# Four feed-forward mixtures of a cross-attention stack: routing, look-ahead and weight spreading rewritten

## The chip, the cores and the metric

The kernel runs on one core of one Trainium2 chip. The metric is device time in microseconds of one execution, the median of several runs. A profiled execution of the same program gives the trace; its own time is named beside it, since every duration below is read from that one execution. Six parts of the core are named: TensorE (PE in the rows, with PEld for its weight loads), VectorE (DVE), ScalarE (ACT), GpSimd (POOL), SyncE (SP), and the DMA queues.

## What is computed

The reference sends 2048 tokens of 128 numbers (x, 8 sequences of 256, float32) through four layers. Each layer is a cross-attention to a context of 8 x 1601 rows, then a feed-forward part; the fourth also has a self-attention in its feed-forward part. The change touches only the four feed-forward mixtures. Three of them are alike:

```python
scores = sigmoid(y @ router_w.T)          # y: the layer norm of x, 16 experts
s = scores + bias                         # 4 groups of 4 experts
# keep the two groups whose two best experts sum highest, then the four best experts in them
w = scores[chosen] / (sum(scores[chosen]) + 1e-20) * SCALE
out = sum over chosen e of  w[e] * (act(y @ gate[e]) * (y @ up[e])) @ down[e]  +  shared part
```

Layer 0 has hidden width 128 per expert and a shared part of 256, layer 1 has 32 and 256, layer 2 has 64 and 128; layers 0 and 1 use silu(gate) * up, layer 2 the square of relu without an up matrix. The fourth takes the one best of 8 experts:

```python
one_hot = one_hot(argmax(y @ gate_w + gate_b))
h = gelu(einsum('td,edh->teh', y, w1))    # hidden 512 per expert
out = einsum('te,ted->td', one_hot, einsum('teh,ehd->ted', h, w2))
```

## The kernel before

The program is nine phases, one behind the other, and each ends before the next begins: L0a, L0f, L1a, L1f, L2a, L2f, L3a, L3s, L3f. The names ending in f are the mixtures. A phase is one block with an instruction list of its own for each engine and its own semaphores, which are cleared behind it (L60). Nothing outside the four mixtures is touched.

A mixture is described by an `Experts` object (L2448) and emitted by `build_experts` (L2494). The tokens are four chunks of 512, each of four token tiles of 128. All weights stay in SBUF, transposed so that an expert's hidden units lie on the 128 partitions. A chunk is worked hidden tile by hidden tile: 18 hidden tiles in L0f (16 routed, 2 shared), 6 in L1f (4 and 2), 9 in L2f (8 and 1), 32 in L3f (4 for each of 8 experts). From here on "tile" is such a hidden tile of 128 units by 512 tokens, one PSUM bank.

For each tile PE makes the first-layer product into `hp` (and the up product into `up`) as three fp32r products, high x high, low x high and high x low (`three`, L2624 to L2626), ACT applies silu, relu or gelu (`hidden`, L2759), DVE multiplies by up (L2969) and by the expert's weight (L2974; L2981 and L2983 in L2f), and PE adds the second-layer product into `yp` as one plain fp32 product (`down`, L2674), which the trace counts as two instructions. PE runs one tile ahead: products(q+1), weigh(q+1), down(q). When a chunk is finished, ACT copies `yp` to `ft` (L2765), PE turns it back (L2620), DVE adds x (L3000) and SP stores it.

The expert's weight is a number per token and has to stand in all 128 partitions. It is cut into three bf16 parts (`cparts`, L2941 to L2946), turned by PE (L2613), copied to `ct` (48 rows: 3 parts of 16 experts, L2951) and spread by a product of `sel` with `ct`, a contraction over 48 rows (`weigh`, L2657; in L3f over 8 rows, `mask`, L2665, applied to the tokens ahead of the first layer by `only`, L2958 and L2959).

Routing of a chunk: DVE takes statistics (L2797 and L2800), an inverse root by shifts and Newton steps of small DVE instructions (L70 to L82, L2808), ACT norms (L2722), PE turns (L2599), ACT copies twice, plain and rounded (L2732, L2733), DVE makes the low part (L2814), PE makes the logits (L2606), ACT the sigmoid (L2741), and DVE picks groups and experts in some 40 small instructions (L2849 to L2946). L1f and L2f route all four chunks first. L0f and L3f route chunk 0 first and the other three beside the tiles of chunk 0, step by step in the order of the table `beside`. The weights are split into high (ACT, L2747 and L2749) and low parts (DVE, L2819 and L2822) before their first use. The order on each engine is the order in which the code is written.

## Time and profile before

| what | us |
|---|---|
| median of three runs (4938.65 to 4943.12) | 4939.88 |
| the profiled execution | 4936.75 |
| its span | 4935.0 |
| TensorE busy in the span | 4338.2 (88%) |
| VectorE, ScalarE, GpSimd busy | 2831.2, 2570.1, 32.7 |
| mean granted TensorE clock, share of full | 0.935 |
| L0f, L1f, L2f, L3f (first transfer to the copy of the last chunk) | 264.9, 126.7, 143.3, 262.0 |

The mixtures begin at 260.9, 1288.0, 3084.1 and 4665.7. Together they are 797 of 4935 us; the attention phases hold the rest. Within a mixture the engines hand tiles to one another, so what sets its length is read from the order of starts on PE, not from the busy shares. In the rows, `128x512 f32` behind a name is the shape of the output, `<-` reads "made from" (or, in brackets, "waited for"), and `x4` counts instructions.

### The profile page before, as it was taken

What the parts mean: (1) busy time and instruction counts of PE and PEld (TensorE: products, weight loads), DVE (VectorE), ACT (ScalarE), POOL (GpSimd) and SP (SyncE); (2) the same over time, 40 slices, a digit from 0 to 9 for tenths busy, and PEclk for the clock granted to TensorE, in tenths of its full rate; (3) what the DMA queues carried; (4) which work ended last, traced back from release to release, by engine and by line L of the source; (5) the groups of instructions that cost most, each with busy time, mean ns of one, the idle gap of its engine ahead of it and who ended that gap; (6) DMA issues with size and microseconds to landing.
All of it is one profiled execution on the core that took longest, in us unless ns stands there. A gap on an engine that the chain in (4) does not pass through costs nothing. (4 is left out here: it accounts for less than half of the span.)

```text
span 4935.0 us, 76710 instructions
## 1 busy us (share of the span) xinstructions
PE 4338.2 (88%) x27172; PEld 2929.8 (59%) x27172; DVE 2831.2 (57%) x7008; ACT 2570.1 (52%) x4392; POOL 32.7 (1%) x23
## 2 busy tenths in 40 slices
PE   3869799999579999999899998669999999967699
PEld 3635444545357777777677776346666666644455
DVE  6654688888355666556565564555555555447531
ACT  4532377767327666666666665234444444336433
POOL 0000000000000000000000000000000000000000
PEclk8879799999689999999999999789999999988899
DMA  1110143331010000000000000010000000000100
GB/s 46 27 44 7 60 61 45 53 48 28 23 50 2 13 11 6 12 5 13 13 4 11 3 3 2 25 52 9 7 9 8 8 2 2 2 18 4 59 3 7
DMA packets 115142, 99.36 MB, mean 20 GB/s; under 512 B 11480, under 2 KB 106872, under 8 KB 113648
## 3 DMA queue, kind: packets, MB, share of 16 engines
q1 hardware_dynamic: 108992, 87.35, 8.1%
q10 hardware_dynamic: 5760, 6.92, 0.4%
q8 instruction: 232, 3.80, 0.3%
q14 instruction: 158, 1.29, 0.1%
HBM read 62.91 MB, written 12.58 MB: 15 GB/s over the span
## 5 line engine op out<-in xcount | busy, mean ns | idle before, releaser
L1240 DVE CUSTOM_DVE_ANT_0 L2a_sc<-L2a_score,L2a_mask_n 128x804 f32<-128x804 f32 x512 | 499.0, 991 | 105.5 <-issue 82.0
L1157 ACT ACTIVATE L2a_pt<-L2a_ring 128x512 f32<-128x512 f32 x768 | 430.6, 598 | 215.6 <-PE L2a_ring L1054 213.6
L621 ACT ACTIVATE L1a_work<-L1a_ring 128x1024 f32<-128x1024 f32 x416 | 413.3, 1026 | 167.4 <-PE L1a_ring L439 166.9
L741 DVE TENSOR_REDUCE L1a_mx<-L1a_ring 128x2 f32<-128x1024 f32 x384 | 456.6, 1222 | 59.8 <-PE L1a_ring L458 56.0
L2178 PE MATMUL L3a_res<-L3a_probs,L3a_n 128*128 128x512 f32 (+1 forms) x960 | 489.6, 592 | 0.0
L2286 ACT ACTIVATE L3a_probs<-L3a_ring 128x512 f32<-128x512 f32 (+1 forms) x480 | 280.1, 590 | 380.5 <-PE L3a_ring L2069 375.9
L1054 PE MATMUL L2a_ring<-L2a_ident,L2a_sc 128*128 128x128 f32 x3072 | 440.8, 282 | 5.5 <-ACT L2a_sc L1144 1.9
L1144 ACT ACTIVATE L2a_sc<-L2a_sc,L2a_nb 128x1608 f32<-128x1608 f32 x256 | 417.2, 1632 | 0.7 <-DVE L2a_nb L1245 0.7
L2392 DVE TENSOR_REDUCE L3a_mx<-L3a_ring 128x1 f32<-128x402 f32 (+2 forms) x640 | 315.6, 538 | 142.9 <-PE L3a_ring L2147 135.2
L1054 PEld LDWEIGHTS L2a_ring<-L2a_ident,L2a_sc 128*128 128x128 f32 x3072 | 347.2, 143 | 81.0 <-issue 44.4
L1069 PE MATMUL L2a_res<-L2a_pt,L2a_v 128*64 128x256 f32 (+1 forms) x3328 | 373.4, 381 | 1.6 <-ACT L2a_pt L1157 1.6
L1265 DVE SCALAR_TENSOR_TENSOR L2a_k_lo<-L2a_ring,L2a_bk,L2a_k_hi 128x402 fp32r<-128x402 f32 x256 | 161.2, 635 | 328.0 <-ACT L2a_k_hi L1176 326.9
L2067 PE MATMUL L3a_ring<-L3a_q_hi,L3a_kt_hi 128*128 128x512 f32 (+1 forms) x480 | 317.4, 661 | 16.6 <-DVE L3a_q_lo L2405 16.6
L1069 PEld LDWEIGHTS L2a_res<-L2a_pt,L2a_v 128*64 128x64 f32 (+1 forms) x3328 | 233.8, 137 | 133.3 <-issue 20.3
L1037 PE MATMUL L2a_score<-L2a_k_hi,L2a_q_hi 64*128 64x402 f32 x1024 | 211.0, 403 | 51.0 <-DVE L2a_mx L1240 36.6
L479 PE MATMUL L1a_res<-L1a_work,L1a_v 128*32 128x256 f32 (+1 forms) x3328 | 229.0, 390 | 3.2 <-ACT L1a_oraw L625 1.7
L1176 ACT ACTIVATE L2a_k_hi<-L2a_ring,L2a_bk 128x402 fp32r<-128x402 f32 x256 | 152.3, 598 | 130.7 <-PE L2a_ring L1018 128.0
L458 PE MATMUL L1a_ring<-L1a_keys,L1a_queries 64*128 64x512 f32 (+1 forms) x1024 | 199.9, 418 | 13.3 <-DVE L1a_mx L741 11.7
L439 PE MATMUL L1a_ring<-L1a_shifted,L1a_keys 64*128 64x512 f32 x832 | 189.3, 462 | 11.4 <-issue 5.8
L2068 PE MATMUL L3a_ring<-L3a_q_lo,L3a_kt_hi 128*128 128x512 f32 (+1 forms) x480 | 189.3, 394 | 0.0
L2069 PE MATMUL L3a_ring<-L3a_q_hi,L3a_kt_lo 128*128 128x512 f32 (+1 forms) x480 | 189.3, 394 | 0.0
L1037 PE MATMUL L2a_score<-L2a_k_hi,L2a_q_lo 64*128 64x402 f32 x1024 | 186.1, 352 | 0.0
(726 smaller groups left out, 8170.7 us busy)
## 6 DMA issues: line engine op xcount, KB each, us to landing
L1a_keys<-L1a_k_hi SPq DMA_DIRECT2D x224, 52.0 KB
...
```

Of the source, the lines that this page charges most:

```text
L621: act.activation(probs[:, (par * NU + u) % c.PS, :, :], ring[tile][:, :, :], ACT.Exp).then_inc(tile_free[tile], 1)
L741: dve.tensor_reduce(mx[:, g % 2, hf, one, :, ch], ring[tile][:, :, :], AX, ALU.max).then_inc(tile_free[tile], 1)
L1037: mm = pe.matmul(score[e][:, k, 0:CH], mine[rows, p % 2, q], theirs[rows, p % 2, w], start=(i == 0), stop=(i == 2))
L1054: mm = pe.transpose(bank[:, t * P:(t + 1) * P], sc[:, r % 2, g // 3, at:at + P], ident[:, :])
L1069: mm = pe.matmul(res[e * DH:(e + 1) * DH, 0:S], v[0:rows, t, h * DH:(h + 1) * DH], pt[0:rows, t, e, :], start=(t == 0), stop=(t == CT - 1))
L1144: act.activation(sc[:, r % 2, e, :], sc[:, r % 2, e, :], ACT.Exp, bias=nb[:, r % 2, e:e + 1], scale=1.0, accum_out=sums[:, r // 2 % 2, r % ...
L1157: ins = act.activation(pt[:, t:t + 4, g // 3, q], bank[:, :].rearrange("p (t q) -> p t q", t=4), ACT.Copy)
L1240: dve.tensor_tensor_reduce(sc[:, two, e, w].rearrange("p (k j) -> p k j", k=2), score[e][:, :, 0:CH], mask_n[:, r % 2, w].rearrange("p (k ...
L2067: pe.matmul(out, hi, m_hi, start=True, stop=False)
L2178: pe.matmul(res[s][:, 0:W], n[0:r, b % c.n_bufs, t, :], probs[0:r, (u * T + i) % c.PS, 0:W], start=first, stop=last).then_inc(pv_ok, 1)
L2286: free(act.activation(probs[0:r, at % c.PS, 0:W], bank[0:r, 0:W], ACT.Exp), "scores", k)
L2392: free(dve.tensor_reduce(mx[:, u % 2, part, to:to + 1], bank[:, 0:valid(s, ch)], AX, ALU.max), "tops", k)
```

## The change

- All 16 token tiles are routed at once before the first weight is spread, in L0f too. Statistics, norm and turns run chunk behind chunk; the turns go to four different PSUM banks, and the 16 logits products follow together.
- The layer norm's inverse root goes from DVE to GpSimd: an add and a power of -0.5 for each chunk (`rsqrt_chunk`). The norm goes from ACT to DVE as a subtract and multiply.
- PE makes the first-layer products of nine tiles (A = 9) before the first spread. DVE's gating multiplies for these nine stand between the routing steps and write into a ring `hid` of 11 tiles; the multiply by the weight follows in place later. L2f has four `hp` banks.
- The first 18 tiles of L0f and 12 of L1f and L2f use plain fp32 products (`w1`, `wu`, `yt`), the others the three fp32r ones, so the splitting comes later.
- `cparts`, `ct` and `sel` have 128 rows, zeroed by GpSimd, so a spread contracts over 128 rows.
- In the weights' scale two DVE instructions become one. The table of the activation function is loaded by a one-column activation ahead.
- L3f has a class and a function of their own (`Single`, `build_single`): three tiles ahead, four `hp` banks, small transfers ahead of `w1`, each chunk's norm and turn beside chunk 0, and from chunk 1 on the second layer as three fp32r products, for which ACT applies gelu twice (rounded to `hid_hi` and plain) and DVE makes `hid_lo`.

```diff
+def rsqrt_chunk(pool, st, half, span):
+    pool.tensor_scalar(st["var"][:, span], st["mv"][:, span, 1], EPS, None, ALU.add)
+    pool.drain()
+    return pool.tensor_tensor(st["rs"][:, span], st["var"][:, span], half[:, span], ALU.pow)
+def norm_chunk(dve, y, x, st, tiles):
+    for t in tiles:
+        ins = dve.tensor_scalar(y[:, t, :], x[:, t, :], st["mv"][:, t, 0:1], st["rs"][:, t:t + 1], ALU.subtract, ALU.mult)
...
-        sel_f, sel = sb("sel_f", [3 * E, c.SEL, P]), sb("sel", [3 * E, c.SEL, P], BF16)
+        sel_f, sel = sb("sel_f", [W, c.SEL, P]), sb("sel", [P, c.SEL, P], BF16)
-        g1, hid = sb("g1", [P, 2, CHUNK]), sb("hid", [P, 2, CHUNK])
+        g1, hid = sb("g1", [P, 2, CHUNK]), sb("hid", [P, R, CHUNK])
...
+            pe.wait_ge(c_in, 16 * 3)
+            for n in range(CN):
+                turn(n)
+            logits()
+            for q in range(A):
+                products(q)
+            parts(0)
+            parts(1)
+            weigh(0)
             for q in range(Q):
-                if q + 1 < Q:
-                    products(q + 1)
-                    weigh(q + 1)
+                if q + A < Q:
+                    products(q + A)
+                if q + 1 < Q:
+                    weigh(q + 1)
                 down(q)
...
+                if plain:
+                    pe.matmul(hp[q % NB][:, :], w1[:, k, :], yt[:, n, :], start=True, stop=True).then_inc(hp_ok, 1)
-                pe.matmul(wp[q % 2][:, :], sel[0:W, k // c.share, :], ct[:, n, :], start=True, stop=True).then_inc(wp_ok, 1)
+                pe.matmul(wp[(r - 1) % 2][:, :], sel[:, k // c.share, :], ct[:, n, :], start=True, stop=True).then_inc(wp_ok, 1)
...
+            groups()
+            gate(0)
+            second()
+            gate(1)
+            keep()
+            gate(2)
...
+            cast()
+            for q in range(7, A):
+                gate(q)
+            parts(0)
+            parts(1)
+            hidden(0)
+            for q in range(Q):
+                if q + A < Q:
+                    gate(q + A)
+                if q + 1 < Q:
+                    hidden(q + 1)
...
+                if n == 0:
+                    pe.wait_ge(hid_ok, q + 1)
+                    pe.matmul(yp[:, :], w2[:, k, :], hid[:, q % 2, :], start=first, stop=last).then_inc(dn_ok, 1)
+                    return
+                pe.wait_ge(lo_ok, q - KC + 1)
+                pe.matmul(yp[:, :], w2_hi[:, k, :], hid_hi[:, q % R, :], start=first, stop=False)
+                pe.matmul(yp[:, :], w2_lo[:, k, :], hid_hi[:, q % R, :], start=False, stop=False)
+                pe.matmul(yp[:, :], w2_hi[:, k, :], hid_lo[:, q % R, :], start=False, stop=last).then_inc(dn_ok, 1)
```

On PE, from the logits of L0f's first chunk to its first down product (`misc` is a PSUM bank for turns and logits, `w` the gate and down weights), the order before was:

```order
L2606 MATMUL L0f_misc<-L0f_wr,L0f_yt 128x16 x4
L2624 MATMUL L0f_hp<-L0f_yt_hi,L0f_w_hi 128x512
L2625 MATMUL L0f_hp<-L0f_yt_hi,L0f_w_lo 128x512
L2626 MATMUL L0f_hp<-L0f_yt_lo,L0f_w_hi 128x512
L2624 MATMUL L0f_up<-L0f_yt_hi,L0f_wu_hi 128x512
...
L2613 MATMUL L0f_misc<-L0f_ident_b,L0f_cparts 48x128 x4
L2657 MATMUL L0f_wp<-L0f_ct,L0f_sel 128x512
...
L2657 MATMUL L0f_wp<-L0f_ct,L0f_sel 128x512
L2674 MATMUL L0f_yp<-L0f_hid,L0f_w 128x512
```

and in the changed kernel:

```order
L2588 MATMUL L0f_misc<-L0f_wr,L0f_yt 128x16 x16
L2623 MATMUL L0f_hp<-L0f_yt,L0f_w 128x512
L2629 MATMUL L0f_up<-L0f_yt,L0f_wu 128x512
...
L2594 MATMUL L0f_misc<-L0f_ident_b,L0f_cparts 128x128 x8
L2594 MATMUL L0f_yp<-L0f_ident_b,L0f_cparts 128x128 x8
L2642 MATMUL L0f_wp<-L0f_ct,L0f_sel 128x512
L2623 MATMUL L0f_hp<-L0f_yt,L0f_w 128x512
L2629 MATMUL L0f_up<-L0f_yt,L0f_wu 128x512
L2642 MATMUL L0f_wp<-L0f_ct,L0f_sel 128x512
L2655 MATMUL L0f_yp<-L0f_hid,L0f_w 128x512
```

The logits of all four chunks, nine tiles' products (the dots stand for eight further pairs) and all 16 turns of the parts now stand ahead of the first spread, and each first-layer product is one instruction in place of three; nine tiles lie between a tile's products and its down product.

On DVE, in L0f's routing (`choice` to `gsum` are the group sums, `g` is ACT's output), the order before was:

```order
L2849 TENSOR_TENSOR L0f_choice<-L0f_score,L0f_rb 128x64
...
L2862 TENSOR_TENSOR L0f_gsum<-L0f_first,L0f_two 128x16
L2868 TENSOR_TENSOR L0f_g_large<-L0f_gsum 128x8
...
L2969 TENSOR_TENSOR L0f_hid<-L0f_up,L0f_g 128x512
L2974 TENSOR_TENSOR L0f_hid<-L0f_wp,L0f_hid 128x512
```

and in the changed kernel:

```order
L2789 TENSOR_TENSOR L0f_choice<-L0f_score,L0f_rb 128x256
...
L2801 TENSOR_TENSOR L0f_gsum<-L0f_first,L0f_two 128x64
L2869 TENSOR_TENSOR L0f_hid<-L0f_up,L0f_g 128x512
L2806 TENSOR_TENSOR L0f_g_large<-L0f_gsum 128x32
...
L2812 TENSOR_TENSOR L0f_thr<-L0f_thr,L0f_wsum 128x16
L2869 TENSOR_TENSOR L0f_hid<-L0f_up,L0f_g 128x512
L2774 TENSOR_TENSOR L0f_g_above<-L0f_gsum,L0f_thr 128x64
```

The routing steps now work on all 16 token tiles at once (256 columns for 64), the gating multiply of one tile stands behind each of them, and the multiply by the weight follows elsewhere.

On PE, in L3f's loop (before: chunk 0, the later chunks alike; `ym` the masked tokens), the order before was:

```order
L2665 MATMUL L3f_wp<-L3f_ct,L3f_sel 128x512
L2674 MATMUL L3f_yp<-L3f_hid,L3f_w 128x512
L2624 MATMUL L3f_hp<-L3f_ym_hi,L3f_w_hi 128x512
L2625 MATMUL L3f_hp<-L3f_ym_hi,L3f_w_lo 128x512
L2626 MATMUL L3f_hp<-L3f_ym_lo,L3f_w_hi 128x512
```

and in the changed kernel, in chunk 1:

```order
L3090 MATMUL L3f_hp<-L3f_ym_hi,L3f_w_hi 128x512
L3091 MATMUL L3f_hp<-L3f_ym_hi,L3f_w_lo 128x512
L3092 MATMUL L3f_hp<-L3f_ym_lo,L3f_w_hi 128x512
L3078 MATMUL L3f_wp<-L3f_ct,L3f_sel 128x512
L3108 MATMUL L3f_yp<-L3f_hid_hi,L3f_w_hi 128x512
L3109 MATMUL L3f_yp<-L3f_hid_hi,L3f_w_lo 128x512
L3110 MATMUL L3f_yp<-L3f_hid_lo,L3f_w_hi 128x512
```

The down product is three fp32r products from the rounded and the low part of `hid`.

## Rows read from the trace of the kernel before

**Rows 1.** the four phases by stretch: length, then busy PE, PEld, DVE, ACT, POOL; clock; DMA

```profile
255.00:531.00 276.00, 222.68 (x728) 126.55 (x727) 137.12 (x328) 71.27 (x118) 0.00 (x0) 0.88 0.07 23
1285.00:1420.00 135.00, 82.61 (x288) 51.10 (x288) 58.65 (x172) 32.51 (x64) 0.00 (x0) 0.74 0.09 26
3081.00:3234.00 153.00, 94.48 (x292) 48.62 (x292) 78.01 (x197) 37.81 (x72) 0.00 (x0) 0.76 0.08 24
4663.00:4935.00 272.00, 231.33 (x752) 130.58 (x752) 68.96 (x163) 95.33 (x164) 0.00 (x0) 0.93 0.09 28
```

**Rows 2.** the copy of each finished chunk: ns min/median/max, first to last start

```profile
L2765 ACT ACTIVATE L0f_ft<-L0f_yp x4: 597/598/598, 377.6 to 525.8; 128x512 f32<-128x512 f32 x4
...
L2765 ACT ACTIVATE L1f_ft<-L1f_yp x4: 597/598/598, 1365.8 to 1414.7; 128x512 f32<-128x512 f32 x4
...
L2765 ACT ACTIVATE L2f_ft<-L2f_yp x4: 597/598/600, 3166.5 to 3227.4; 128x512 f32<-128x512 f32 x4
...
L2765 ACT ACTIVATE L3f_ft<-L3f_yp x4: 598/598/599, 4765.5 to 4927.7; 128x512 f32<-128x512 f32 x4
```

**Rows 3.** one tile of L0f on PE, with and without the spread (start, us)

```profile
443.57 0.39 PE L2626 MATMUL L0f_up<-L0f_yt_lo,L0f_wu_hi 128*128 128x512 f32 x1
443.89 0.39 PE L2657 MATMUL L0f_wp<-L0f_ct,L0f_sel 48*128 48x512 bf16 x1
...
445.40 0.40 PE L2625 MATMUL L0f_hp<-L0f_yt_hi,L0f_w_lo 128*128 128x512 f32 x1
...
471.17 0.39 PE L2626 MATMUL L0f_up<-L0f_yt_lo,L0f_wu_hi 128*128 128x512 f32 x1
471.40 1.02 PE L2674 MATMUL L0f_yp<-L0f_hid,L0f_w 128*128 128x512 f32 x2
...
472.49 0.40 PE L2625 MATMUL L0f_hp<-L0f_yt_hi,L0f_w_lo 128*128 128x512 f32 x1
```

**Rows 4.** the token tiles' transfers and statistics in L0f, L1f and L2f

```profile
L2576 SPq DMA_DIRECT2D L0f_x<-x_L0a x3: 428/507/527, 261.9 to 262.9; - x3
...
DMA to landing us min/median/max: 2.9/9.7/11.4
...
L2797 DVE BATCH_NORM_STATS2 L1f_st_six<-L1f_x x16: 274/276/295, 1293.4 to 1298.9; 128x6 f32<-128x128 f32 x16
...
L2797 DVE BATCH_NORM_STATS2 L2f_st_six<-L2f_x x16: 275/278/294, 3090.0 to 3095.5; 128x6 f32<-128x128 f32 x16
```

**Rows 5.** timeline rows of the setup and routing, and L101 by its line

```profile
4675.81 0.23 DVE L3015 CAST L3f_ident_b<-L3f_ident 128x128 bf16<-128x128 f32 x1 [9.67 <-DMA L3f_bx<-in_L3f_bx]
...
4680.54 0.16 DVE L2808 SCALAR_TENSOR_TENSOR L3f_st_off<-L3f_st_mv,L3f_st_rs 128x4 f32<-128x4 f32 x1
...
L101 DVE TENSOR_SCALAR L2a_xn<-L2a_xin,L2a_st_mv,L2a_st_rs x16: 341/342/346, 1441.5 to 2777.6; 128x128 f32<-128x128 f32 x16
...
1311.33 1.86 PE L2606 MATMUL L1f_misc<-L1f_wr,L1f_yt 128*128 128x16 f32 x8 [5.10 <-ACT L1f_yt_hi L2733]
...
1327.34 0.42 DVE L2849 TENSOR_TENSOR L1f_choice<-L1f_score,L1f_rb 128x256 f32<-128x256 f32 x1 [1.57 <-ACT L1f_score L2741]
...
1342.66 0.29 DVE L2946 CAST L1f_cparts<-L1f_comb 128x256 bf16<-128x256 f32 x1
```

**Rows 6.** one turn of the chain in L2f, all engines

```profile
3181.17 0.40 PE L2626 MATMUL L2f_hp<-L2f_yt_lo,L2f_w_hi 128*128 128x512 f32 x1
...
3181.61 0.60 ACT L2759 ACTIVATE L2f_g<-L2f_hp 128x512 f32<-128x512 f32 x1 [1.47 <-PE L2f_hp L2626]
...
3182.24 0.69 DVE L2981 TENSOR_TENSOR L2f_hid<-L2f_wp,L2f_g 128x512 f32<-128x512 f32 x1 [0.60 <-ACT L2f_g L2759]
```

**Rows 7.** L3f, the down product of its second tile on PE

```profile
4701.71 1.02 PE L2674 MATMUL L3f_yp<-L3f_hid,L3f_w 128*128 128x512 f32 x2
```

**Rows 8.** the stretch in which L1f routes, columns as in Rows 1

```profile
1320.00:1345.00 25.00, 8.77 (x34) 6.77 (x34) 15.09 (x62) 5.05 (x11) 0.00 (x0) 0.50 0.00 0
```

**Rows 9.** the costliest GpSimd instruction of the program, by line

```profile
L669 POOL TENSOR_TENSOR L1a_rq_wide<-L1a_rq,L1a_one 128x1024 f32<-128x1024 f32 x8 | 15.2, 1906 | 721.8 <-DVE L1a_rq L768 721.8
```

More of the change, by code:

```diff
@@ L2456, in __init__ @@
         self.share = max(1, routed // E)
-        self.PARTS = 1 if top1 else 3
-        self.batches = [(0, N_CHUNK)] if second is None else [(0, 1), (1, N_CHUNK)]
-        self.pieces = [(0, 2), (2, (2 + tiles) // 2), ((2 + tiles) // 2, tiles)]
-        chunks = range(1, N_CHUNK)
-        steps = [("stats", n) for n in chunks] + [("rsqrt", 1)] + [("norm", n) for n in chunks]
-        for n in chunks:
-            steps += [("turn", n), ("logits", n)]
-        steps += [(s, 1) for s in (("best", "cast") if top1 else ("groups", "second", "keep", "masked", "top", "pick", "weights",
-                                                                 "cast"))]
@@ L2466, in __init__ @@
-        steps += [("parts", n) for n in chunks]
-        self.beside = {q: [] for q in range(tiles)}
-        if second is not None:
-            for i, s in enumerate(steps):
-                self.beside[1 + i * (tiles - 3) // (len(steps) - 1)].append(s)
-        self.misc = []
-        for c0, c1 in self.batches[:1]:
-            for n in range(c0, c1):
-                self.misc += [("turn", n), ("logits", n)]
-            self.misc += [("parts", n) for n in range(c0, c1)]
-        for q in range(N_CHUNK * tiles):
-            n, k = divmod(q, tiles)
-            if k == 1 and n:
-                self.misc.append(("back", n - 1))
-            if n == 0:
-                self.misc += [s for s in self.beside[k] if s[0] in ("turn", "logits", "parts")]
@@ L2482, in __init__ @@
-        self.misc.append(("back", N_CHUNK - 1))
+        self.pieces = [(k, min(k + 6, tiles)) for k in range(0, tiles, 6)]
+        self.NF = plain // tiles
+        self.matrices = 2 if act == "silu" else 1
+        self.lows = [("low", i) for i in range(len(self.pieces))] + [("turn_lo", n) for n in range(self.NF, N_CHUNK)]
 EXPERTS = {
-    "L0f": Experts("L0f", 16, 18, 16, "silu", fill=-1.0, scale=2.5, second=True),
-    "L1f": Experts("L1f", 16, 6, 4, "silu", fill=LOWEST),
-    "L2f": Experts("L2f", 16, 9, 8, "relu2", fill=0.0, scale=2.5),
@@ L2489, with stats_chunk @@
-    "L3f": Experts("L3f", 8, 32, 32, "gelu", top1=True, second=True),
+    "L0f": Experts("L0f", 16, 18, 16, "silu", -1.0, 2.5, 9, 18),
+    "L1f": Experts("L1f", 16, 6, 4, "silu", LOWEST, 1.0, 9, 12),
+    "L2f": Experts("L2f", 16, 9, 8, "relu2", 0.0, 2.5, 9, 12),
 }
 G = 4
-def build_experts(nc, c, io, x_in, x_out, x_more=None):
-    E, KC, KR, CN = c.E, c.KC, c.KR, N_CHUNK
+def stats_chunk(dve, x, st, tiles):
+    for t in tiles:
+        dve.bn_stats(st["six"][:, t, :], x[:, t, :])
+    dve.drain()
+    for t in tiles:
+        ins = dve.bn_aggr(st["mv"][:, t, :], st["six"][:, t, :])
+    return ins
@@ L2558, in build_experts @@
         span_of = lambda n: slice(n * CTILES, (n + 1) * CTILES)
[L2559 to L2568 removed]
+        routed = lambda q: q % KC < KR
+        routed_to = lambda q: sum(1 for r in range(q + 1) if routed(r))
+        piece_of = lambda k: next(i for i, (p0, p1) in enumerate(c.pieces) if p0 <= k < p1)
         block = done.enter_context(nc.Block())
@@ L3003, in finish, with residual @@
                 dve.nop().then_inc(xo_ok, 1)
-            steps = dict(stats=stats, rsqrt=rsqrt, turn=turn, groups=groups, second=second, keep=keep, masked=masked_of, top=top,
-                         pick=pick, weights=weights, best=best, cast=cast, parts=parts)
+            def residual(n):
+                dve.wait_ge(more_in, 16 * CN)
+                dve.tensor_tensor(more[:, span_of(n), :], more[:, span_of(n), :], x[:, span_of(n), :], ALU.add)
+            steps = dict(stats=stats, norm=norm, turn=turn, best=best, parts=parts)
             dve.memset(seg[:, :, :], 1.0)
```

887 lines of the change are left out of this document (548 added, 339 removed).

## The prediction, made before the changed kernel was run

> **What bounds the kernel now.** I read the stretches of the four phases first [rows 1]. They show where PE is short of work: in L0f it is busy 222.7 of 276 us, in L3f 231.3 of 272, but in L1f only 82.6 of 135 and in L2f 94.5 of 153, at granted clocks of 0.74 and 0.76. No other engine comes near its stretch in L1f (DVE 58.7). So there are two kinds of time: a head, in which one engine waits for the next until routing is done, and a body, in which PE (L0f, L3f) or the chain ACT-DVE-PE (L2f) sets the pace. Then the copies that end each chunk [rows 2]: they fix the end of each phase's PE work (525.8, 1414.7, 3227.4, 4927.7) and of L0f's and L3f's first chunk (377.6, 4765.5). I forecast each phase's last down product against these ends; what follows it (copy, turn, add, store) is the same before and after. Last come single tiles on PE [rows 3], the head's rows [rows 4, 5] and the chain [rows 6].
>
> **Prices on PE at full clock** [rows 3]. One fp32r product: 471.17 to 471.40, 0.23; three are 0.69. From the last up product of one tile to the second product of the next takes 472.49 - 471.17 = 1.32 without a spread, which leaves 1.32 - 2 x 0.23 = 0.86 for a plain fp32 product. The same stretch with a spread takes 445.40 - 443.57 = 1.83, so the spread over 48 rows costs 0.51, more than twice an fp32r product of as many columns. A gated routed tile is 1.38 + 0.51 + 0.86 = 2.75 before. Chunks 1 to 3 of L0f come out at 16 x 2.75 + 2 x 2.24 + about 1.5 for turning back = 50.0 each, and the rows give (525.8 - 377.6) / 3 = 49.4 [rows 2], so the prices hold.
>
> **The spread over 128 rows.** No row of before has a bf16 product of 128 rows beside fp32r ones. Nearest from below: 0.23, as any 512-column product. From above: 0.51, unchanged, if the step between number types is what costs it and not the step between row heights. I take 0.23, because the plain down product (also another type) shows no such extra in [rows 3]. The Trainium skill, "TensorEngine Tiling (Array Packing)", section Key Properties, says that a change of tiling mode drains the TensorE; it would explain 0.51 and its removal, and no row of before shows a 48-row product without the change. By that rule the sum is the one below, without it the rival B.
>
> **The head.** The changed DVE list runs four statistics and four norms before the last turn. Statistics: 5.5 us from the first to the last start of four chunks [rows 4], some 1.6 a chunk with the copy and its drain that the change drops, so 1.35. Norm on DVE: 16 instructions of 0.34 on the same shape [rows 5], 1.2 a chunk against some 1.9 on ACT. Inverse root: on DVE it lies between 4675.81 and 4680.54, where twelve small instructions and the statistics take 4.7 [rows 5]; on GpSimd I take under 1 us, hidden for all but the first chunk, with no row of that operation (bounds: 0.3, and the 1.9 of a 1024-column multiply [rows 9]; a price beyond these is rival D). The logits, four times 1.86 at the low clock [rows 5], are 7.4, and turn and copy of the last chunk 1.1. So the logits are done x1 + 1.35 + 4.8 + 2.7 + 0.25 + 1.1 + 7.4 = x1 + 17.6, with x1 the landing of the second chunk's tokens. Choice to last cast for 16 tiles takes 1342.66 + 0.29 - 1327.34 = 15.6 [rows 5]; the change leaves out one of these steps (0.25) and adds seven gating multiplies of about 0.65, and the sigmoid 0.5. I add 1.6 for DVE waiting on cold products: a plain pair at half clock is 2 x 1.72 = 3.4 and a routing step with its gate about 2.9, L1f being granted 0.50 while it routes [rows 8]. Two sets of turned parts and copies take 2.2. PE then runs on end from F = x1 + 41.9. The high and low parts of the weights now lie beside this; DVE and ACT have room, since a tile takes 1.4 and 0.6 of them against PE's 2.5.
>
> **L0f.** x1: issued from 261.9, landing after 9.7 [rows 4], 271.6, so F = 313.5. Left on PE: 9 plain tiles 15.5, 54 tiles at 1.38 = 74.5, 72 down products 61.9, 63 spreads 14.5, three turns back 1.5, and 1.8 of small gaps: 169.7. End 483.2 against 525.6: **-42.4**. Of it 17.6 (63 x 0.28) is from the spreads; the rest is chunk 0, which ended 377.6 - 261.9 = 115.7 after the tokens' issue, where another chunk took 49.4 [rows 2, 4].
>
> **L1f.** Chunk 0's statistics began at 1293.4 [rows 4]; the second chunk is issued a microsecond later, x1 = 1294.4, F = 1336.3. Left: 3 plain tiles 5.2, 12 x 1.38 = 16.6, 24 x 0.86 = 20.6, 15 spreads 3.5, 1.8 for turns and gaps: 47.7. End 1384.0 against 1414.5: **-30.5**.
>
> **L2f.** x1 = 3090.0 - 0.1 by the same reading, F = 3131.8. Here PE has 1.8 a tile, and a chain is longer: from the start of the last product's pass at 3181.17 ACT starts 0.44 later, DVE 0.63 after that [rows 6]; gate and weight multiply are 0.69 each with drains, so 2.4 from the pass's end to the down product, then 0.86 and 0.69 on PE. That round of 3.93 serves two tiles, since two gates are always under way: 1.96 a tile. 27 tiles so make 53.1, the last nine at about 1.1 (0.86 + 0.23) 9.9, turns and a cold start 2.6: 65.6. End 3197.4 against 3227.2: **-29.8**.
>
> **L3f.** Before, the first instruction waits 9.67 for a 512-byte transfer queued behind w1 [rows 5], and the second down product starts at 4701.71 [rows 7]. After, small transfers go first (I take 4 sooner), statistics and root lie ahead of that landing (4.7), the norm is 0.7 shorter, and two conversions leave the path (1.8): 11.2 earlier. Chunk 0 loses about 6 us of stalls with four hp banks and three tiles ahead, so it ends at 4748.3 instead of 4765.4: -17.1. Chunks 1 to 3: 32 x (0.69 + 0.69) + 8 x 0.23 + 0.5 = 46.5 each, less 2.1 at the end where no products are left: 137.4 against 162.2 [rows 2]: -24.8. ACT's two gelus take 1.2 and DVE 1.0 a tile, both under 1.44, so they stay hidden; a tile more than that would show. Together **-41.9**.
>
> **Sum.** 42.4 + 30.5 + 29.8 + 41.9 = 144.6. Five semaphores more in each of three phases to clear cost about 0.7: -143.9. The profiled execution took 4936.75, its span 4935.0, so 4792.8; the median lies 3.1 above that execution: 4796.
>
> **The rivals.** (A) As above, 4796; single prices move it between 4782 and 4812. (B) The 128-row spread keeps its 0.51: 63 x 0.28 in L0f, 15 in L1f, some 3 us in L2f where a chain hides part of it, and 32 in L3f make 34: 4829. For it: bf16 stands beside fp32r in either kernel. Against it: the plain product's own switch is free. (C) PE is granted half its clock through head and early body, since it is idle between the nine products: L1f's 0.50 while routing [rows 8] speaks for it, L0f's 0.88 [rows 1] against it. Plain tiles at 3.4 would make DVE wait 0.5 at each of seven gates and the products after F slow at first; 4 to 5 us in each of four phases: 4812 to 4816. (D) Slower than before: the power on GpSimd. With p us a call, three phases wait about 4p - 5 longer each and L3f p - 1, together 13p - 16. It takes back 144 us from p = 12.3 on, 4940 and more. GpSimd's only shown price is 1.9 for 1024 columns [rows 9], and this has four. The Trainium skill, "GPSIMD Engine Reference", section Instruction dispatch, gives about 6 us once for the first call of a freshly loaded kernel; here that would fall into the wait for x. (E) The head is shorter than my stalls and the body without gaps: 4778. (F) A cover fails and the look-ahead doesn't help (say DVE's ring waits tie it to PE): only the spreads and L3f are gained, about 4885.
>
> **How the numbers follow.** A 0.60, B 0.15, C 0.12, E 0.07, F 0.03, D 0.03. The range 4771 to 4836 takes in A, B, C and E. A measurement of this kernel can tell about 0.2% (10 us) from no change. Faster by more than that are A, B, C, E and F, 0.97; slower is D from 12.3 us a call, of which I leave 0.02; within 0.2% 0.01.
>
> **What would show it.** In the changed trace: L0f's chunks 1 to 3 between copies at about 45 us (16 x 2.47 + 2 x 2.24 + 1.5) where B gives 49.5; from the last up pass to the down product's start over a spread 0.46 where B gives 0.6 to 0.7; the first down product at about 313, 1336 less the earlier phase's gain, and so on; L2f's down products every 1.96 on the mean; L3f's every 1.44, its ACT never waited for. GpSimd's power under 1 us. Wrong would be the forecast above all if the head of L1f and L2f, where I claim half their gain, waits for something that no row here shows: the second batch of turns on `yp` and `wp`, the table loads, or the zeroing of `cparts` by GpSimd.

## The result and the profile after

The changed kernel takes 4788.05 us (median of 4 runs, 4786.25 to 4795.74), the kernel before 4939.37 beside it (4938.65 to 4943.12). The ratio is 0.9695, 95% interval [0.9678, 0.9712]: 151 us or 3.1% faster. Forecast were 4796 and a range of 4771 to 4836. The profiled execution took 4788.48, its span is 4786.7.

The stretches of [rows 1] begin 3 to 6 us before their mixture and end 5 to 7 after its last copy. Cut to the mixtures themselves, from the first transfer to the last copy, they read in the kernel before (length, then busy time of PE, PEld, DVE, ACT and POOL, granted clock, DMA share, GB/s):

```profile
260.90:525.80 264.90, 221.05 (x716) 125.36 (x716) 135.23 (x323) 70.67 (x117) 0.00 (x0) 0.88 0.07 23
1288.00:1414.70 126.70, 81.95 (x284) 50.68 (x284) 57.96 (x171) 31.92 (x63) 0.00 (x0) 0.74 0.08 26
3084.10:3227.40 143.30, 93.82 (x288) 48.20 (x288) 77.32 (x196) 37.25 (x72) 0.00 (x0) 0.76 0.08 24
4665.70:4927.70 262.00, 230.67 (x748) 130.17 (x748) 68.27 (x162) 94.77 (x164) 0.00 (x0) 0.93 0.09 28
```

and in the changed one:

```profile
261.30:480.90 219.60, 199.01 (x669) 116.56 (x680) 127.19 (x261) 56.05 (x92) 9.03 (x12) 0.92 0.09 27
1247.10:1344.80 97.70, 79.58 (x257) 45.12 (x260) 56.20 (x160) 24.12 (x40) 7.72 (x12) 0.84 0.11 33
3001.80:3117.10 115.30, 87.38 (x272) 45.91 (x276) 75.78 (x189) 30.04 (x52) 8.18 (x12) 0.84 0.10 29
4553.40:4779.40 226.00, 205.97 (x829) 150.12 (x844) 134.46 (x246) 139.40 (x250) 7.90 (x12) 0.94 0.10 33
```

PE's busy time in L0f fell from 221.1 to 199.0 us, but the phase fell more, from 264.9 to 219.6: PE now works 91% of it in place of 83%. In L1f it is 81% in place of 65%, in L2f 76% in place of 65%, and the granted clock of the two rose from 0.74 and 0.76 to 0.84. In L3f PE's share rose least, from 88% to 91%.

The changed kernel's issue of the first token transfer of each mixture (ns, then start), and below it the copies of the finished chunks, which answer to [rows 2]:

```profile
L2564 SPq DMA_DIRECT2D L0f_x<-x_L0a x1: 363/363/363, 261.3 to 261.3; - x1
...
L2564 SPq DMA_DIRECT2D L1f_x<-x_L1a x1: 382/382/382, 1247.1 to 1247.1; - x1
...
L2564 SPq DMA_DIRECT2D L2f_x<-x_L2a x1: 378/378/378, 3001.8 to 3001.8; - x1
...
L3024 SPq DMA_DIRECT2D L3f_x<-x_L3s x1: 359/359/359, 4553.4 to 4553.4; - x1
```

The copies, ns min/median/max, then first to last start:

```profile
L2708 ACT ACTIVATE L0f_ft<-L0f_yp x4: 597/599/599, 359.3 to 480.9; 128x512 f32<-128x512 f32 x4
...
L2708 ACT ACTIVATE L1f_ft<-L1f_yp x4: 597/598/604, 1310.7 to 1344.8; 128x512 f32<-128x512 f32 x4
...
L2708 ACT ACTIVATE L2f_ft<-L2f_yp x4: 597/598/599, 3068.6 to 3117.1; 128x512 f32<-128x512 f32 x4
...
L3181 ACT ACTIVATE L3f_ft<-L3f_yp x4: 597/604/617, 4641.8 to 4779.4; 128x512 f32<-128x512 f32 x4
```

From first transfer to the last chunk's copy L0f takes 480.9 - 261.3 = 219.6 us, where it took 525.8 - 260.9 = 264.9; the others follow in the table.

| gain, us | forecast | measured |
|---|---|---|
| L0f: 264.9 to 219.6 | 42.4 | 45.3 |
| L1f: 126.7 to 97.7 | 30.5 | 29.0 |
| L2f: 143.3 to 115.3 | 29.8 | 28.0 |
| L3f: 262.0 to 226.0 | 41.9 | 36.0 |
| the four together | 144.6 | 138.3 |
| all that lies between and around them | -0.7 | 10.0 |
| spans: 4935.0 to 4786.7 | 143.9 | 148.3 |

So the sum came out 4 us short, by two errors that partly cancel: the mixtures gained 6 less than forecast, which is L3f's miss, since the errors of the other three nearly cancel among themselves, and what the change doesn't touch became 10 shorter. The experiments take up both.

### The profile page after: what moved, and what is told of

It reads as the page before. It is cut to its first block and busy times, and to the rows that moved or that the text cites. A ratio compares the mean times of both kernels' runs of the same rounds, so it can differ in the third digit from the quotient of the medians.

```text
span 4786.7 us, 76756 instructions
## 1 busy us (share of the span) xinstructions
PE 4280.6 (89%) x27163; PEld 2929.6 (61%) x27196; DVE 2885.7 (60%) x7012; ACT 2585.6 (54%) x4410; POOL 65.6 (1%) x71
## 5 line engine op out<-in xcount | busy, mean ns | idle before, releaser
L1037 PE MATMUL L2a_score<-L2a_k_hi,L2a_q_hi 64*128 64x402 f32 x1024 | 207.3, 396 | 41.9 <-DVE L2a_mx L1240 35.6
L2178 PEld LDWEIGHTS L3a_res<-L3a_probs,L3a_n 128*128 128x128 f32 (+1 forms) x960 | 175.2, 189 | 18.0 <-issue 1.0
```

Of the source, the lines that this page charges most:

```text
L2178: pe.matmul(res[s][:, 0:W], n[0:r, b % c.n_bufs, t, :], probs[0:r, (u * T + i) % c.PS, 0:W], start=first, stop=last).then_inc(pv_ok, 1)
```

## The spread over 128 rows

One tile of L0f on PE in the changed kernel, with its spread (`wp`), answering to the first three rows of [rows 3]:

```profile
360.27 0.40 PE L2608 MATMUL L0f_up<-L0f_yt_lo,L0f_wu_hi 128*128 128x512 f32 x1
360.51 0.39 PE L2642 MATMUL L0f_wp<-L0f_ct,L0f_sel 128*128 128x512 bf16 x1
360.74 1.02 PE L2655 MATMUL L0f_yp<-L0f_hid,L0f_w 128*128 128x512 f32 x2
...
361.83 0.39 PE L2607 MATMUL L0f_hp<-L0f_yt_hi,L0f_w_lo 128*128 128x512 f32 x1
```

The spread now takes 0.23 (360.51 to 360.74), as the fp32r products of 512 columns beside it do. From the last up product to the second product of the next tile it is 361.83 - 360.27 = 1.56, where it was 1.83 with the same instructions. Two experiments take the change apart. Most experiments had one run; their readings rest on the lengths of the phases in the trace.

**The changed kernel with 48 rows again.**

```diff
-                pe.matmul(wp[(r - 1) % 2][:, :], sel[:, k // c.share, :], ct[:, n, :], start=True, stop=True).then_inc(wp_ok, 1)
+                pe.matmul(wp[(r - 1) % 2][:, :], sel[0:W, k // c.share, :], ct[0:W, n, :], start=True, stop=True).then_inc(wp_ok, 1)
...
-                pe.matmul(wp[u % 2][:, :], sel[:, e, :], ct[:, n, :], start=True, stop=True).then_inc(wp_ok, 1)
+                pe.matmul(wp[u % 2][:, :], sel[0:E, e, :], ct[0:E, n, :], start=True, stop=True).then_inc(wp_ok, 1)
```

> The changed kernel, but each spread contracts over 48 rows again (8 in L3f); everything else stays. Theory: the height of the contraction costs 0.28 us a spread where PE sets the pace, so L0f is longer by 63 x 0.28 = 17.6 us, L1f by 15 x 0.28 = 4.2, L3f by up to 32 x 0.28 = 9 and L2f by 0 to 3, together 31 to 34. Rival: the changed surroundings of the spread (look-ahead) made it short, and the height costs nothing: under 3 us in all.

One tile of L0f on PE in this kernel, start and length in us, with its 48-row spread:

```profile
400.03 0.39 PE L2608 MATMUL L0f_up<-L0f_yt_lo,L0f_wu_hi 128*128 128x512 f32 x1
400.35 0.39 PE L2642 MATMUL L0f_wp<-L0f_ct,L0f_sel 48*128 48x512 bf16 x1
400.67 1.12 PE L2655 MATMUL L0f_yp<-L0f_hid,L0f_w 128*128 128x512 f32 x2
...
401.87 0.40 PE L2607 MATMUL L0f_hp<-L0f_yt_hi,L0f_w_lo 128*128 128x512 f32 x1
```

It took 4824.2 us in one run, 36 more than the changed kernel. By phase: L0f 236.8 (+17.2), L1f 101.6 (+3.9), L2f 118.1 (+2.8), L3f 232.6 (+6.6), together 30.5, just under the 31 expected; the rest is in L1a, of which more below. In the rows of PE the price has three parts: 0.32 ahead of the spread and 0.32 behind it, in place of 0.23 or 0.24 each, and 401.87 - 400.67 = 1.20 in place of 1.09 from the down product on. So PE loses about a tenth of a microsecond at each of the two crossings between heights and another tenth on the product behind the second.

**The kernel before with 128 rows only.**

```diff
-        sel_f, sel = sb("sel_f", [3 * E, c.SEL, P]), sb("sel", [3 * E, c.SEL, P], BF16)
+        sel_f, sel = sb("sel_f", [3 * E, c.SEL, P]), sb("sel", [P, c.SEL, P], BF16)
...
-        ct = sb("ct", [W, CN, CHUNK], BF16)
+        ct = sb("ct", [P, CN, CHUNK], BF16)
...
-                pe.matmul(wp[q % 2][:, :], sel[0:W, k // c.share, :], ct[:, n, :], start=True, stop=True).then_inc(wp_ok, 1)
+                pe.matmul(wp[q % 2][:, :], sel[:, k // c.share, :], ct[:, n, :], start=True, stop=True).then_inc(wp_ok, 1)
...
+            dve.memset(sel[:, :, :], 0.0)
+            dve.memset(ct[:, :, :], 0.0)
```

(the copies into `sel` and `ct` still fill the first 48 rows, and L3f's mask product is changed in the same way)

> The kernel before, with only the spreads made 128 rows high (zeroed rows in sel and ct). Theory (height costs 0.28 a spread): L0f's chunks 1 to 3 shorter by 16 x 0.28 = 4.5 each, L1f and L3f by 3 to 9, together 25 to 33 faster than before. Rival (the spread is only cheap beside nine tiles of look-ahead): under 5.

The spread on PE in this kernel's L0f, from the last up product to the second product of the next tile:

```profile
430.92 0.40 PE L2626 MATMUL L0f_up<-L0f_yt_lo,L0f_wu_hi 128*128 128x512 f32 x1
431.16 0.39 PE L2657 MATMUL L0f_wp<-L0f_ct,L0f_sel 128*128 128x512 bf16 x1
431.39 1.02 PE L2674 MATMUL L0f_yp<-L0f_hid,L0f_w 128*128 128x512 f32 x2
...
432.48 0.39 PE L2625 MATMUL L0f_hp<-L0f_yt_hi,L0f_w_lo 128*128 128x512 f32 x1
```

It took 4926.15 in one run, 15 less than the 4941.3 beside it, while the phases gain 14.6 (L0f), 1.7 (L1f), 2.1 (L2f) and 9.5 (L3f), 27.9 in all. The same stretch of instructions takes 432.48 - 430.92 = 1.56 where it took 1.83 before, and 1.84 in place of 1.56 when the changed kernel goes back to 48 rows: 0.27 and 0.28. By the lengths of L0f's chunks 1 and 2 a spread is 0.26 cheaper there and 0.29 dearer here. The price is the same in both surroundings within 0.03, so the rival falls, and the height is shown to be the cause: type, count and place of PE's instructions are alike. Against the trace of before (span 4935.0, here 4924.4) only 10.6 of the 27.9 are left, because L1a took 775.0 in this execution and 762.2 in that one, and the other phases 4.5 more in all. The Trainium skill, "TensorEngine Tiling (Array Packing)", section Key Properties, says that a change of tiling mode drains the TensorE. It doesn't say that a product over 48 rows counts as such a change, and no run here shows a drain as such; the rows fit it if it does, and put 0.28 us on a 48-row product between two full ones.

## The head: routing, look-ahead and the root on GpSimd

L0f's head in the changed kernel: GpSimd's power for the first chunk, the second chunk's statistics, the logits, the choice, the last cast, and the first product of the body:

```profile
265.98 1.04 POOL L2484 TENSOR_TENSOR L0f_st_rs<-L0f_st_var,L0f_half 128x4 f32<-128x4 f32 x1 [0.15 <-issue]
...
271.54 0.87 DVE L2474 BATCH_NORM_STATS2 L0f_st_six<-L0f_x 128x6 f32<-128x128 f32 x4 [6.03 <-DMA L0f_x<-x_L0a]
...
281.53 6.85 PE L2588 MATMUL L0f_misc<-L0f_wr,L0f_yt 128*128 128x16 f32 x32
...
288.83 0.43 DVE L2789 TENSOR_TENSOR L0f_choice<-L0f_score,L0f_rb 128x256 f32<-128x256 f32 x1 [7.14 <-ACT L0f_score L2715]
...
309.48 0.29 DVE L2856 CAST L0f_cparts<-L0f_comb 128x256 bf16<-128x256 f32 x1
...
312.23 1.02 PE L2623 MATMUL L0f_hp<-L0f_yt,L0f_w 128*128 128x512 f32 x2 [0.79 <-DVE L0f_ct L2861]
```

The forecast gives 271.6 for the second chunk's tokens, 281.8 for the first logit, 289.8 for the choice, 311.3 for the end of the last cast (309.8 here) and 313.5 for the body's first product. GpSimd's power on four columns takes 1.04 to 1.13, not under 1, and with its add 1.4 to 1.5; it stands beside DVE's next statistics and shows once in DVE's list behind the second chunk, as 0.35 us ahead of the last norm.

**Three tiles ahead in place of nine.**

```diff
-    "L0f": Experts("L0f", 16, 18, 16, "silu", -1.0, 2.5, 9, 18),
+    "L0f": Experts("L0f", 16, 18, 16, "silu", -1.0, 2.5, 3, 18),
```

(likewise L1f and L2f; gates 3 to 6 leave the routing, and ACT's later roundings follow the third tile)

> The changed kernel with three tiles ahead in place of nine in L0f, L1f and L2f (ring of five). Theory (the look-ahead fills PE while DVE routes): six plain tiles of 1.72 come back on PE in L0f and L1f and six of 0.86 in L2f, less four gates of 0.65 that leave the routing chain: +7.7, +7.7, +2.6, together about 18 slower than the changed kernel, with the same pitch of a tile in the body. Rival (PE works the nine tiles at half clock and DVE waits for them, so little is gained): under 5 slower, routing over sooner by more than 4 us in each phase.

The stretch in which L0f routes, in the changed kernel:

```profile
286.00:314.00 28.00, 24.77 (x69) 11.70 (x70) 20.35 (x69) 13.25 (x21) 0.00 (x0) 0.84 0.00 0
```

and with three tiles ahead (columns as in the first stretches above):

```profile
286.00:314.00 28.00, 16.17 (x51) 9.51 (x51) 16.99 (x64) 9.91 (x15) 0.00 (x0) 0.65 0.00 0
```

It took 4805.44 in one run, 17 more. L0f 229.4 (+9.8), L1f 105.0 (+7.3), L2f 117.2 (+1.9), 19.0 together, where the theory had 7.7, 7.7 and 2.6. PE does 16.2 us of work in the 28 of the routing, against 24.8, at a granted clock of 0.65 against 0.84.

Each phase can be split where its body's first product starts. From there to the last copy 10.5, 10.2 and 3.9 us come back in L0f, L1f and L2f, for six plain tiles whose price is 10.3, 10.3 and 5.2. The head in turn is shorter without the four gates. In L0f this hardly shows from the first transfer (the last cast starts at 47.6 in place of 48.1), but the second chunk's statistics began 0.8 later in that execution (11.0 in place of 10.2 after the first transfer), and counted from them the last cast starts 1.4 sooner in L0f, 2.4 in L1f and 2.1 in L2f. Four gates of 0.65 were put at 2.6. So the look-ahead is paid for with 1.4 to 2.4 us of a longer routing, the rival's 4 isn't reached, and the work filled into the wait is the gain, at its price at full clock.

**The inverse root back on DVE.**

```diff
-            for n in range(CN):
-                pool.wait_ge(mv_ok, n + 1)
-                rsqrt_chunk(pool, st, half, span_of(n)).then_inc(rs_ok, 1)
...
+            def root(n):
+                t = span_of(n)
+                dve.drain()
+                dve.tensor_copy(st["var"][:, t], st["mv"][:, t, 1])
+                dve.drain()
+                rsqrt_steps(dve, st["rs"][:, t], st["var"][:, t], st["tmp"][:, t], CTILES)
```

> The changed kernel with the layer norm's inverse root back on DVE, four times 13 small instructions in each phase. Theory (GpSimd's 1.4 us a chunk lies beside DVE's statistics): each chunk adds about 3.3 us to DVE's list ahead of the last turn, of which 0.4 was waited anyway; the three phases with one routing are 11 to 13 longer each and L3f about 2, together 35 to 41 slower. Rival (the logits or the turns bound the head): under 10 slower.

It took 4836.3 in one run, 48 more. L0f +14.2, L1f +13.8, L2f +12.7, L3f +4.2: 44.9, where 35 to 41 were expected. A chunk's round on DVE is 5.63 in place of 2.45 (from one chunk's statistics to the next's), the 3.2 that the theory had, three times over; the last chunk's root comes on top of them, and none of it is hidden. This is the largest single part that an experiment took out. It isn't a gain over before of that size, since the kernel before did the root once or twice a phase on all its chunks, not four times; it is what the chunk-by-chunk head costs without GpSimd.

## L3f: where six microseconds went

The second down product of L3f begins 4577.2 - 4553.4 = 23.8 after the first transfer, where it was 4701.71 [rows 7] - 4665.7 = 36.0. That is 12.2 sooner (forecast 11.2). Chunks 1 to 3 take 137.6 (forecast 137.4). Chunk 0 takes 64.6 from that down product to its copy, and took 63.8 before: the 6 us of stalls that I took off are all still there. In the kernel before this stretch of chunk 0 read:

```profile
4701.70:4765.50 63.80, 58.28 (x209) 32.75 (x208) 19.02 (x59) 26.72 (x52) 0.00 (x0) 1.00 0.00 1
```

PE was idle 5.5 of 63.8 us there, at full clock. The waits of L3f's chunk 0 (engine and line, whom it waited for, us in total, times, longest), and its stretch, in the changed kernel:

```profile
ACT L3f_hid L3175 <- PE L3f_yp L3103: 37.4, 30, 4.8
...
PE L3f_misc L3055 <- ACT L3f_yt_hi L3150: 5.0, 3, 2.2
...
4575.00:4642.00 67.00, 60.63 (x215) 36.16 (x216) 32.43 (x76) 30.92 (x52) 3.80 (x6) 0.95 0.00 0
```

PE is idle 6.4 of these 67 us. ACT waits 30 times for a down product. `hid` has two buffers, so gelu of tile q+3 waits for the down product of tile q+1, and the four `hp` banks hold finished products that nobody may take. ACT's list has the later chunks' turns behind those gelus, and PE waits for them at the logits (5.0 us).

**Four hid buffers.**

```diff
-        hid, hid_hi, hid_lo = sb("hid", [P, 2, CHUNK]), sb("hid_hi", [P, R, CHUNK], F32R), sb("hid_lo", [P, R, CHUNK], F32R)
+        hid, hid_hi, hid_lo = sb("hid", [P, R, CHUNK]), sb("hid_hi", [P, R, CHUNK], F32R), sb("hid_lo", [P, R, CHUNK], F32R)
...
-                if q >= KC + 2:
-                    act.wait_ge(lo_ok, q - KC - 1)
-                elif q >= 2:
-                    act.wait_ge(dn_ok, q - 1)
+                if q >= KC + R:
+                    act.wait_ge(lo_ok, q - KC - R + 1)
+                elif q >= R:
+                    act.wait_ge(dn_ok, q - R + 1)
```

(and the index of `hid` goes from `q % 2` to `q % R` on PE, ACT and DVE)

> The changed kernel with four hid buffers in place of two in L3f. Theory (ACT's gelu waits for the down product two tiles back, so the turns of the later chunks on ACT come late and PE waits for them): chunk 0 of L3f is 4 to 6 us shorter, the waits of ACT for the down product go, chunks 1 to 3 stay at 137.6. Rival (the stalls are the low clock after the start and the late splitting of w1): under 1 us.

The same wait of ACT and the stretch of chunk 0 with four buffers:

```profile
ACT L3f_hid L3175 <- PE L3f_hp L3092: 21.1, 22, 1.5
...
4582.00:4639.00 57.00, 56.85 (x217) 34.28 (x215) 32.44 (x76) 30.14 (x51) 3.80 (x6) 1.00 0.00 0
```

L3f takes 216.4 in place of 226.0, all of the 9.6 in chunk 0 (78.8 against 88.4 from the first transfer), more than I expected. ACT's wait for the down product is gone, it now waits for products, and PE is busy 56.9 of 57 us at full clock. So the buffer was the cause. Of the 10 us between the two stretches 6.2 are PE's idle time, which are the forecast's 6, and 3.8 are its work, done at a granted clock of 1.00 in place of 0.95; that the clock stays up because PE is no longer idle is argued, no run separates the two. The median is 4780.96 (4773.67 to 4785.36), ratio 0.9666 [0.9649, 0.9682], which still touches the changed kernel's interval; the phase's length is what shows the gain.

**The down product plain in all chunks** (on top of the four buffers).

```diff
-                if n == 0:
+                if True:
                     pe.wait_ge(hid_ok, q + 1)
                     pe.matmul(yp[:, :], w2[:, k, :], hid[:, q % R, :], start=first, stop=last).then_inc(dn_ok, 1)
                     return
...
-                if q >= KC:
-                    if q >= KC + R:
-                        act.wait_ge(dn_ok, q - R + 1)
-                    act.activation(hid_hi[:, q % R, :], hp[q % 4][:, :], ACT.Gelu_apprx_tanh)
...
-                if q + A >= KC and q + A < Q:
-                    lower(q + A)
```

> As e5_hid4, but L3f's down product is one plain fp32 product in all chunks, so no hid_hi, no hid_lo and one gelu a tile. Theory (a plain product is 0.86, three fp32r 0.69): chunks 1 to 3 are 96 x 0.17 = 16 us longer. Rival (two gelus a tile and the low part cost as much in waits as the products save): within 4 us.

Two down products on PE in a later chunk of this kernel:

```profile
4680.72 1.02 PE L3103 MATMUL L3f_yp<-L3f_hid,L3f_w 128*128 128x512 f32 x2
...
4682.27 1.02 PE L3103 MATMUL L3f_yp<-L3f_hid,L3f_w 128*128 128x512 f32 x2
```

It took 4790.18 in one run, against the median of 4780.96 with four buffers alone. Chunks 1 to 3 take 154.4 in place of 137.6: 16.8 more, 0.175 for each of 96 tiles, and a tile without a mask is 4682.27 - 4680.72 = 1.55 long in place of the 1.38 of six fp32r products. These are PE's own prices, so the two gelus and the low part are hidden.

## L2f: the chain and its cause

The body ran at about 2.0 us a tile (chunks 1 and 2 take 18.4 each for nine tiles with one turn-back), a little over the forecast's 1.96. Two down products, and DVE's two multiplies between them, in the changed kernel:

```profile
3081.94 1.02 PE L2655 MATMUL L2f_yp<-L2f_hid,L2f_w 128*128 128x512 f32 x2
...
3082.54 0.69 DVE L2869 TENSOR_TENSOR L2f_hid<-L2f_hp,L2f_g 128x512 f32<-128x512 f32 x1 [0.76 <-ACT L2f_g L2702]
...
3083.32 0.69 DVE L2876 TENSOR_TENSOR L2f_hid<-L2f_wp,L2f_hid 128x512 f32<-128x512 f32 x1
...
3084.07 0.30 PEld L2655 LDWEIGHTS L2f_yp<-L2f_hid,L2f_w 128*128 128x128 f32 x2 [0.85 <-DVE L2f_hid L2876]
```

The down product at 3084.07 waited for the multiply by the weight (L2876), which stood in DVE's list behind a gate (L2869) that waited for ACT and so for PE's newest product. The nine tiles of look-ahead don't help there, because the list ties the oldest tile to the youngest. The forecast has this chain; what it doesn't say is that the order of two lines makes it.

**The two turned round in L2f.**

```diff
-                if q + A < Q:
+                if gated and q + A < Q:
                     gate(q + A)
                 if q + 1 < Q:
                     hidden(q + 1)
+                if not gated and q + A < Q:
+                    gate(q + A)
```

> The changed kernel with DVE's list in L2f turned round in the loop: the multiply by the weight of tile q+1 ahead of the gate of tile q+9. Theory (L2f's 2.01 us a tile is the chain product, relu, gate, weight, down, made by that order): PE sets the pace at 0.69 + 0.23 + 0.86 = 1.78, so L2f is 27 x 0.23 = 6 us shorter. Rival (DVE's and ACT's own work with their drains is the bound): under 1 us.

Two down products of L2f in this kernel, with DVE's weight multiply and gate between them:

```profile
3082.85 1.02 PE L2655 MATMUL L2f_yp<-L2f_hid,L2f_w 128*128 128x512 f32 x2
3083.05 0.69 DVE L2876 TENSOR_TENSOR L2f_hid<-L2f_wp,L2f_hid 128x512 f32<-128x512 f32 x1 [0.47 <-PE L2f_wp L2642]
...
3083.66 0.68 DVE L2869 TENSOR_TENSOR L2f_hid<-L2f_hp,L2f_g 128x512 f32<-128x512 f32 x1
...
3084.64 1.05 PE L2655 MATMUL L2f_yp<-L2f_hid,L2f_w 128*128 128x512 f32 x2
```

A tile now takes 3084.64 - 3082.85 = 1.79, PE's own 0.69 + 0.23 + 0.86. L2f takes 108.6 in place of 115.3, 6.7 less; the total was 4785.65 in one run.

**Both finds together.**

> The changed kernel with both finds: four hid buffers in L3f and the turned order in L2f. If they are independent, L3f is 9.6 us shorter and L2f 6.7, so 16 us less than the changed kernel's 4788: about 4772. If one hides in the other or in what follows, under 12 less.

L2f 108.8 and L3f 216.7, so they add up in the trace. The median is 4772.88 (4760.86 to 4784.76, 5 runs), ratio 0.9653 [0.9639, 0.9667], which lies wholly under the changed kernel's interval. It is the fastest version here, 15 us under the changed kernel by the medians.

## What the unchanged phases did

Of the 10 us outside the mixtures, L2a alone made 12.4 (1669.4 from L1f's last copy to L2f's first transfer before, 1657.0 after), L1a took 4.0 back and the rest, L3a and L3s above all, gave 1.6. Twice in L2a, where its loop comes round, PE stands idle and the profile names nothing that it waited for. PE's waits of that kind in L2a (us in total, times, longest), in the kernel before:

```profile
PE L2a_score L1037 <- issue: 14.3, 2, 7.5
```

and in the changed one:

```profile
PE L2a_score L1037 <- issue: 6.2, 2, 3.3
```

One of them before: PE's last product, the issue of the next context's transfer by SP, PE's next product:

```profile
2044.89 0.40 PE L1018 MATMUL L2a_ring<-L2a_wv_lo,L2a_kt_hi 128*128 128x512 f32 x1
...
2047.13 0.37 SPq L956 DMA_DIRECT2D L2a_cx<-in_ctx  x1
...
2052.80 0.70 PE L1037 MATMUL L2a_score<-L2a_k_hi,L2a_q_hi 64*128 64x402 f32 x2 [7.52 <-issue]
```

I took this for PE fetching instructions beside the context's 768 KB, longer or shorter by where its list lies. The trace bears out the first half. One of its DMA queues is named `instruction`, and this is what it moved in the stretch of that wait, from 2045.0 to 2053.0 (transfers, MB, share of 16 engines), in the kernel before:

```profile
q8 instruction: 2, 0.03, 1.8%
```

and in the first of the two waits in the changed kernel, from 1973.3 to 1976.9:

```profile
q8 instruction: 1, 0.02, 2.3%
```

A transfer of this queue is 16 KB. In 27 of the 28 waits of this kind in the fourteen traces one begins within 0.1 us of the end of PE's last product, in the other 0.4 behind it; where PE waits 2.9 to 3.4 us there is one, where it waits 6.8 to 7.5 there is a second, 4.1 to 4.8 behind the first. So PE waits for one or two loads of its instructions, as far as timing can show it. What is open is why the old form needs two.

Three kernels moved the lists by empty instructions at the start of L0f, 64 each on PE, ACT and DVE, then 120, 49 and 73, then 136 on PE alone. The first of them:

```diff
+            for _ in range(64 if c.name == "L0f" else 0):
+                pe.nop()
```

> The kernel before with 64 empty instructions on each of PE, ACT and DVE at the start of L0f, where they wait for tokens; nothing else. It asks why the unchanged phase L2a is 12 us shorter in the changed kernel. Theory (where an instruction list falls in memory decides how long PE waits for its instructions at the turn of L2a's loop beside a context transfer): L2a's length moves by over 2 us, and PE's longest waits there from 7.5. Rival (the length follows from the data's or the clock's state left by L1f): L2a stays within 1 us of before.

> The changed kernel with 120 empty instructions on PE, 73 on DVE and 49 on ACT at the start of L0f, so that L2a begins about as many instructions into each list as in the kernel before (64 more on all three moved nothing there). Theory (the place of the lists decides PE's wait for instructions at the turn of L2a's loop): L2a goes from 1657 back to 1665 to 1672 and PE's two waits there from 3.3 to about 7. Rival (it isn't the place of these three lists): L2a stays at 1653 to 1661 and the waits at 3.3.

> The kernel before with 136 empty instructions on PE alone at the start of L0f, which puts PE's list where the changed kernel has it, counted in blocks of 256. Theory (PE's own list decides, by its place in a fetched block): L2a 1656 to 1662, PE's waits 3.3. Rival (another engine's list, or the sum of all, or none): L2a 1668 to 1672, waits 7.1 to 7.5.

None moved the waits. L2a was 1668.4 and 1665.4 in the two kernels of the old form (64 on each list, 136 on PE; 4939.07 and 4932.99 in one run each), with PE's two waits 14.2 and 14.1 in all, and 1657.3 with 6.1 in the padded changed one (4795.98 in one run). So the place of PE's list doesn't decide, as far as these three places can show, and this half of the theory falls. The last run put L1f alone in its new form.

> The kernel before with L1f alone in its new form; L0f, L2f and L3f stay old. Theory (the phases add up, each with its own gain): L1f is 97.7 in place of 126.7 and the others stay at 264.9, 143.3 and 262.0 within 2, so 29 us faster: 4911. It also asks whether L1f, which runs just ahead of L2a, is what shortens L2a. If it is: L2a 1653 to 1661, PE's two waits at the loop's turn 3.3, and 10 us more in the total. If not: L2a 1665 to 1672, waits 7.1 to 7.5.

PE's waits of this kind in its L2a:

```profile
PE L2a_score L1037 <- issue: 6.4, 2, 3.3
```

L1f takes 98.4 and the other three keep their lengths within 3.0, where 2 was expected (261.9, 143.0 and 260.3). L2a is 1655.2 with waits of 3.3 and 3.1: it is the new L1f, the phase just ahead, that shortens L2a. The median is 4899.94 (4892.59 to 4905.02) against 4942.77, ratio 0.9914 [0.9897, 0.993], 43 us for a phase that itself gained 28. What in L1f does it is open. The number of L1f's own instructions on every list, its semaphores and its work on GpSimd all differ, and no run here takes one of them alone. PE's two waits explain 8 of the 12.4 us between before and after. The other 4 are PE's busy time in L2a, 1567.9 before and 1563.9 after for the same 11788 instructions, at a granted clock of 0.97 and 0.98. Over all traces L2a took 1653.6 to 1664.5 with the new L1f (ten traces, mean 1657.4; the longest in the run with both finds, at waits of 3.3 and 3.1) and 1665.4 to 1671.9 with the old one (four traces, mean 1668.8).

L1a is another matter. It took 762 to 775 us in the fourteen traces without following any change. Its last sixth was granted 0.95 of full clock in the five shortest (762.2 to 766.5) and 0.90 to 0.94 in the nine from 766.7 on. No run shows whether the clock is the cause of the length or goes with it. A single run's total can't be read to better than that, which is why the phases' lengths stand here.

## The prediction, step by step

**What bounds the kernel now** held: head and body are the right parts, and PE's order of starts gave ends to a few microseconds.

**Prices on PE** held: 0.23, 0.69, 0.86. L0f's chunks 1 and 2 take 44.4, where 16 x 2.47 + 2 x 2.24 + 1.5 = 45.5 was forecast; the turn-back costs 0.4 rather than that line's 1.5. (The sum for L0f has 1.5 for all three of them, so there it is worth only 0.3.)

**The spread** held at 0.23, so B fell. Its unchanged 0.51 would have cost 30.5 by the first experiment where I wrote 34.

**The head** held within 1.6 us at each of its steps in L0f; the chain from choice to the last cast took 20.9, as 15.6 - 0.25 + 7 x 0.65 + 1.6 had it (21.5). Set apart where the body's first product starts, and without the 0.2 from the last product to its copy, the three alike phases compare so:

| us | head, forecast | head, measured | body, forecast | body, measured |
|---|---|---|---|---|
| L0f | 52.6 | 50.9 | 169.7 | 168.5 |
| L1f | 48.3 | 48.1 | 47.7 | 49.4 |
| L2f | 47.7 | 45.8 | 65.6 | 69.2 |

L0f gained 2.9 more than forecast, 1.7 of it in the head. L1f fell short by 1.5, in its body. **L2f** fell short by 1.8, which hides two errors: the head came 1.9 sooner and the body took 3.6 longer. Of these, 2.01 a tile for 1.96 is 1.4, and another 1.4 is one wait of PE for the first low part of the tokens (`yt_lo`), which DVE makes behind its gates and of which no term speaks. Here two errors cancel by luck.

**The other rivals.** C wanted half the clock through head and early body, and 4 to 5 us for it in each phase. While they routed, L0f, L1f and L2f were granted 0.84, 0.85 and 0.70, no head was longer than forecast, and the first 20 us of the bodies had 1.00, 1.00 and 0.95: C fell. GpSimd's power took 1.1 a call, far from the 12.3 at which D decides. E's shorter heads came in L0f and L2f, its body without gaps in neither L1f nor L2f. F fell, since L1f and L2f gained 29.0 and 28.0; that DVE's list ties it to PE is nevertheless what sets L2f's pace.

**L3f** is the step that failed: "Chunk 0 loses about 6 us of stalls with four hp banks and three tiles ahead". It lost none: the stretch took 64.6 where it took 63.8. I counted banks and tiles on PE's side and didn't follow the ring on ACT's side, whose two buffers were unchanged; with four buffers the same stretch takes 54.9. The other terms of L3f held (measured 12.2 for a forecast of 11.2, and 24.6 for 24.8).

**The sum** took phases as independent of what runs ahead of them. They aren't: L2a gave 12.4 that no term had. The total was right to 8 us partly by luck, because this covered L3f's miss. Of the 8, the spans make 4.4; the other 3.5 are that the median lies 0.4 below the profiled execution, where it lay 3.1 above it before.
